# Macaron block on one Trainium2 core: the shared expert moved into the routing stage, routed rows added in a stage of their own, five down passes for the experts

## The reference

```python
x = x + 0.5 * ffn(layernorm(x))
x = x + attention(layernorm(x))
x = x + 0.5 * ffn(layernorm(x))     # the same ffn weights

def ffn(xf):                        # xf: [T, 256]
    scores = sigmoid(xf @ gate_w.T)                 # 8 experts
    w, idx = top_k(scores, 2); w = 2.5 * w / w.sum(-1)
    shared = silu(xf @ shared_wg.T) * (xf @ shared_wu.T) @ shared_wd.T    # 352 hidden units
    h = silu(xf @ exp_wg[e].T) * (xf @ exp_wu[e].T)                       # 176 hidden units per expert
    routed = sum over the two chosen e of w_e * (h @ exp_wd[e].T)
    return shared + routed
```

## Time and profile before

| | us |
|---|---|
| median of 3 runs (lowest, highest) | 1437.1 (1436.49, 1438.13) |
| the profiled execution's own time | 1431.21 |
| its span, first to last instruction | 1429.5 |

### The profile page before, as it was taken

How to read it: one execution, slowest core, us unless ns; L and a number is a source line. 1 busy time by engine, 2 the same in 40 slices (tenths; PEclk the granted TensorE clock), 3 DMA queues, 4 the chain that set the end, 5 groups by cost and what they waited for, 6 DMA issues and landing times. The chain is left out here.

```text
span 1429.5 us, 42640 instructions
## 1 busy us (share of the span) xinstructions
PE 1219.7 (85%) x14356; PEld 938.2 (66%) x14357; DVE 1019.7 (71%) x2317; ACT 770.1 (54%) x1965; POOL 547.7 (38%) x745
## 2 busy tenths in 40 slices
PE   2817999899969849999998999997865299998998
PEld 1516999899958714555554555553743199998998
DVE  6594555479979688898886888981766845554887
ACT  2524556433336504887775777877544156564333
POOL 1555444245524401332332223222535554442554
PEclk9557999999979958999998999999975599998999
DMA  5602433322254492221221222101244034442333
GB/s 184 189 16 76 125 123 122 94 67 73 74 169 166 177 114 52 67 63 59 60 63 49 59 59 64 45 4 35 95 135 135 1 119 124 123 120 76 108 111 106
DMA packets 94745, 132.12 MB, mean 92 GB/s; under 512 B 15040, under 2 KB 79488, under 8 KB 94592
## 3 DMA queue, kind: packets, MB, share of 16 engines
q1 hardware_dynamic: 73088, 85.97, 21.0%
q0 software_dynamic: 13056, 35.67, 9.0%
q10 hardware_dynamic: 8448, 8.39, 1.7%
HBM read 81.35 MB, written 48.23 MB: 91 GB/s over the span
## 5 line engine op out<-in xcount | busy, mean ns | idle before, releaser
L1467 ACT ACTIVATE s_PR<-s_ps_b 128x512 f32<-128x512 f32 (+3 forms) x768 | 331.2, 496 | 144.8 <-PE s_ps_b L1583 139.9
L1489 DVE TENSOR_REDUCE s_MX<-s_ps_a 128x1 f32<-128x512 f32 (+3 forms) x608 | 358.3, 655 | 54.7 <-PE s_ps_a L1558 51.7
L1583 PE MATMUL s_ps_b<-s_QO,s_KO 99*32 99x512 bf16 (+3 forms) x3072 | 220.0, 329 | 9.2 <-issue 4.4
L1443 POOL TENSOR_SCALAR_AFFINE_SELECT s_PR<-s_PR 128x256 f32<-128x256 f32 x256 | 103.0, 405 | 311.6 <-ACT s_PR L1467 305.6
L1558 PE MATMUL s_ps_a<-s_KO,s_QO 96*32 96x512 bf16 (+3 forms) x3072 | 216.4, 339 | 2.7 <-issue 1.7
L604 POOL DMA_INDIRECT f_XG<-xn_scratch,f_tok_u x144 | 136.4, 947 | 165.5 <-PE f_ps_x L701 155.6
L811 POOL DMA_INDIRECT f_YG<-y_scratch,f_slots_u x128 | 121.0, 945 | 143.5 <-DVE X L886 87.9
L1600 PE MATMUL s_ps_o<-s_PR,s_VG 128*17 128x512 f32 (+3 forms) x1536 | 161.1, 488 | 1.0 <-POOL s_PR L1443 0.6
L1583 PEld LDWEIGHTS s_ps_b<-s_QO,s_KO 99*32 99x32 bf16 x3072 | 82.9, 96 | 91.0 <-ACT s_PR L1467 44.7
L657 DVE TENSOR_TENSOR f_xl<-f_ps_x,f_xh 128x256 fp32r<-128x256 f32 x144 | 61.1, 425 | 97.9 <-ACT f_xh L629 97.9
L1558 PEld LDWEIGHTS s_ps_a<-s_KO,s_QO 96*32 96x32 bf16 x3072 | 84.4, 99 | 69.6 <-DVE s_MX L1489 22.7
(11 more groups left out here) (206 smaller groups left out, 3048.9 us busy)
## 6 DMA issues: line engine op xcount, KB each, us to landing
y_scratch<-f_YS SPq DMA_DIRECT2D x144, 128.0 KB, 1.7
qk_scratch<-p_QK SPq DMA_DIRECT2D x32, 384.0 KB, 2.6
s_QO<-qk_scratch SPq DMA_DIRECT2D x96, 128.0 KB, 2.8
s_KO<-qk_scratch SPq DMA_DIRECT2D x96, 128.0 KB, 2.8
xn_scratch<-f_XN ACTq DMA_DIRECT2D x16, 512.0 KB, 3.3
f_stage<-in_w_up SPq DMA_DIRECT2D x20, 352.0 KB
X<-in_x SPq DMA_DIRECT2D x4, 1024.0 KB, 9.4
x_scratch<-X SPq DMA_DIRECT2D x1, 4096.0 KB, 14.8
```

What stands on the lines that cost most here:

```text
L1443: nc.gpsimd.affine_select(out=tile, in_=tile, compare_op=ALU.is_ge, fill=0.0, base=0, pattern=[[0, 2], [1, P]], channel_multiplier=-1)\
L1467: nc.scalar.activation(PR[:, u // 2 % SLOTS, u % 2, 0:W - lo], ps_b[u % RING][:, lo:W], ACT.Exp, scale=SCALE).then_inc(exp_done, 1)
L1489: nc.vector.tensor_reduce(MX[:, h:h + heads, i, s], ps_a[slot][:, 0:heads * keys].rearrange("p (h n) -> p h n", h=heads), AX.X, ALU.max).t ...
L1583: last = nc.tensor.matmul(ps_b[u % RING][strip, lo:W], KO[k][0:RM, h, i * P + strip.start:i * P + strip.stop], QO[k][0:RM, h, hf * W + lo: ...
```

## The change

- The shared expert is computed in the routing stage (now `front_stage`), in the layout "units on partitions, tokens moving": for each wave of four tiles three pieces of 128, 128 and 96 hidden units, each with six passes for gate and six for up of **512 columns** (L716), into a ring of three PSUM banks (`take`). H needs no transposes; ACT and DVE/POOL split it (L381, L339, L507), and nine passes of 256 columns per tile give the result (L730), which DVE adds to X (`add_shared`).
- The gating is spread over waves -1 to 1 (`GATED`), the choice of experts follows in wave 2, the slots in wave 3, and one-hot rounds two to a wave in waves 4 to 7 (`ROWS_AT`). POOL makes no one-hot part any more; ACT makes both (`token_ids`, one instruction of 576 columns and eight of 72).
- The normalised tokens' high and low parts lie in the room of expert w's weights (`x_part`) until wave w's up passes are done; so the weights of expert w are split one wave later (`expert_up`, `expert_down` on ACT, `expert_low` on POOL), from a single staging buffer RAW that SP loads.
- `combine_stage` takes the place of `shared_stage`: only the 64 gathers (ring of eight tiles), two additions per tile, the statistics, and in f2 the stores.
- `expert_stage`: H is cut into 112 and 64 units. The high and the low part of the 64 units lie one above the other on 128 partitions (DVE writes the low part to partitions 64 to 127), and the high weights of those units are kept twice, so low x high and high x high are one pass: five down passes in place of six. DVE makes the low parts in two instructions of 128 columns in place of one of 256.

The core of the diff:

```diff
-        expert_stage(nc, tag, S, ident, WUh, WUl, WDh, WDl, tok_u, unit_i, xn_dram, y_dram)
-        shared_stage(nc, tag, S, X, ST, MV, RSTD, W12, slots_u, ident, WUh, WUl, WSh, WSl, y_dram, out_dram)
+        front_stage(nc, tag, S, X, ST, MV, ident, w_up, w_down, w_shared, gate, xn_dram,
+                    W, RSTD, W12, slots_u, tok_u, unit_i)
+        expert_stage(nc, tag, S, ident, W, tok_u, unit_i, xn_dram, y_dram)
+        combine_stage(nc, tag, S, X, ST, W12, slots_u, y_dram, out_dram)
...
+    GATED = {-1: (0, 1), 0: (2, 3, 4), 1: (5, 6, 7)}
+    LAST_GATED = max(GATED)
+    COUNT_AT = LAST_GATED + 2
+    ROWS_AT = {4: (0, 1), 5: (2, 3), 6: (4, 5), 7: (6, 7)}
...
+            def load_expert(e):
+
+                if e == 0:
+                    sp.wait_ge(shared_lo, 2 + HC)
+                else:
+                    sp.wait_ge(expert_lo, 3 * e)
...
+            for w in range(NW):
+                for m in range(2):
+                    pool.wait_ge(hh_done, HC * w + m + 1)
+                    nc.gpsimd.tensor_tensor(hs[1][:, m, :], H[:, (HC * w + m) % 2, :],
+                                            hs[0][:, m, :].bitcast(F32), ALU.subtract).then_inc(hl_pool, 1)
+                if w >= 1:
+                    expert_low(w - 1)
+            expert_low(NW - 1)
...
+            pe.wait_ge(shared_lo, 2 + HC)
+            for w in range(NW):
+                gated = GATED.get(w, ())
+                up(w, 0)
+                for v in gated[0:1]:
+                    transpose_x(v, 0)
+                    transpose_x(v, 1)
+                for n in ROWS_AT.get(w - 1, ())[1:2]:
+                    tokens(n)
+                if w == COUNT_AT:
+                    counts()
+                if w >= 1:
+                    for i in range(4):
+                        down(w - 1, i)
+                for v in gated[0:1]:
+                    logits(v)
+                for v in gated[1:2]:
+                    transpose_x(v, 0)
+                    transpose_x(v, 1)
+                up(w, 1)
+                for v in gated[0:1]:
+                    turn_logits(v)
+                for v in gated[1:2]:
+                    logits(v)
+                for v in gated[2:3]:
+                    transpose_x(v, 0)
+                    transpose_x(v, 1)
+                up(w, 2)
+                for v in gated[1:2]:
+                    turn_logits(v)
+                for v in gated[2:3]:
+                    logits(v)
+                    turn_logits(v)
+                for n in ROWS_AT.get(w, ())[0:1]:
+                    tokens(n)
+            for i in range(4):
+                down(NW - 1, i)
+            tokens(7)
...
-                plan = split_passes(2)
-                for i, (c, a, b) in enumerate(plan):
-                    last = nc.tensor.matmul(ps_y[k % 2][:, 0:D], hs[a][:, k % 2, c * P:(c + 1) * P],
-                                            W_down[b][c][:, ds((unit - NS) * D, D)],
+                plan = ((hh[0:FA, b, 0:P], S.AH), (hh[0:FA, b, 0:P], S.AL), (hl[:, b, :], S.AH),
+                        (hh[:, b, P:2 * P], S.BH), (hh[0:FB, b, P:2 * P], S.BL))
...
+                if t >= RING:
+                    pool.wait_ge(x_done, t - RING + 1)
```

More of the change, by code:

```diff
@@ L101, in sb @@
             return ctx.enter_context(nc.sbuf_tensor(f"{tag}_{name}", shape, dt))
[L103 to L108, removed]
+        W = sb("W", [P, E, S.BLOCK], F32R)
         RSTD = sb("RSTD", [P, NT])
@@ L437, in _, with place @@
                                                         ALU.mult, ALU.mult))
+            def place():
                 dve.wait_ge(pre_copied, 2)
@@ L537, in _ @@
                 pe.wait_ge(sel_done, 1)
                 pe.wait_ge(consts, 6)
+                take("count", 0)
                 sel = SEL[:, :, :].rearrange("p e t -> p (e t)")
@@ L541, in _ @@
                 nc.tensor.matmul(ps_count[:, 1, :], ones_b[:, :], sel, start=True, stop=True).then_inc(pre_done, 1)
-                for n in range(8):
-                    pe.wait_ge(rows, n + 1)
-                    pe.wait_ge(par_ids, n + 1)
-                    pe.wait_ge(tile_ids, n + 1)
-                    for g in range(CH):
-                        last = nc.tensor.matmul(ps_tok, RSEL[:, n % 2, g, :],
-                                                TSEL[:, n % 2, g, :, :].rearrange("p a j -> p (a j)"),
-                                                start=n == 0 and g == 0, stop=n == 7 and g == CH - 1)
-                    last.then_inc(tok_done, 1)
@@ L553, in feed_forward, with tokens @@
-        expert_stage(nc, tag, S, ident, WUh, WUl, WDh, WDl, tok_u, unit_i, xn_dram, y_dram)
-        shared_stage(nc, tag, S, X, ST, MV, RSTD, W12, slots_u, ident, WUh, WUl, WSh, WSl, y_dram, out_dram)
+            def tokens(n):
+                pe.wait_ge(rows, n + 1)
+                pe.wait_ge(ids, n + 1)
+                for g in range(CH):
+                    last = nc.tensor.matmul(ps_tok, RSEL[:, n % 2, g, :],
+                                            TSEL[:, n % 2, g, :, :].rearrange("p a j -> p (a j)"),
+                                            start=n == 0 and g == 0, stop=n == 7 and g == CH - 1)
+                last.then_inc(tok_done, 1)
@@ L736, in _ @@
             U = 12
+            pe.wait_ge(cleared, 2)
             transpose_x(0, 0)
@@ L988, in attention @@
+                    nc.vector.bn_stats(ST[:, t, :], X[:, t, :])
+            for t in range(NT + 2):
+                if t < NT:
+                    add(t, 0)
+                if 1 <= t <= NT:
+                    add(t - 1, 1)
+                if t >= 2:
+                    statistics(t - 2)
 def attention(nc, S, X, ST, MV, ident, w_qkv, b_qk, b_v, w_out, b_out):
```

1050 lines of the change are left out of this document (531 added, 519 removed).

## The result

| | before | changed |
|---|---|---|
| median of 4 runs, us (lowest, highest) | 1437.62 (1436.49, 1438.33) | 1566.47 (1564.51, 1570.66) |
| ratio, 95% interval | | 1.0901 (1.0875 to 1.0927) |
| profiled execution, us (span) | 1431.21 (1429.5) | 1567.95 (1567.5) |

Slower, as forecast, but by 129 us where I said 82, and 4.5 us above the top of my range. The changed kernel's windows by stage answer to the earlier trace rows; in order: routing, experts and combine of f1, then of f2. Columns: window, its length, busy time of PE, of its weight loads, DVE, ACT and POOL with their counts, clock, DMA share, GB/s.

A forecast was written before the change was run, and what follows sets the result against it. PE was taken to bound the expert and shared stages, DVE chains the routing stage. 175.5 - 16.8 - 76.9 = +81.8 us gave a span of 1511, execution 1513 and, with 5.9 added, median 1519; range 1468 to 1562.

The forecast's parts named there:

- Step 1: Expert stages: one 256-column down pass less in each of 72 tiles at 0.116 us, 8.4 us less per feed-forward.
- rival C: Expert stages: the fifth pass gives nothing because DVE's low parts come late; 16.8 us lost, 1536; chance 0.05.
- Step 2: Combine stage replacing the shared stage, bound by POOL's gathers: 84.7 us in f1 (-38.9), 86.1 in f2 (-38.0).
- Step 3: Routing stage with the shared expert's work: 186.5 us in sum, +88.2 in f1, +87.3 in f2; bounds 150 and 214.
- Waits: Routing stage: PE waiting on chains of other engines, 32 us in sum.
- counts: Routing stage: PE's wait for the choice of experts ahead of the counts, 6 us.
- wave 3 to 4: Routing stage: PE's wait while DVE work stands behind the 11 us slots chain, 9 us.
- rounds: Routing stage: PE's waits for the ids of one-hot rounds 1, 3 and 5, 3 us each, 9 in all.
- Low clock: Routing stage: PE at reduced clock, 4 us at the start and 2 us after its waits.
- The tail: End of the routing stage: 7 us to load and split expert 7, then 1.9 to the first gather; 9 us.
- rival B: Routing stage: the clock falls in the waits, 14 to 30 us more per feed-forward, 1547 to 1579; chance 0.17.
- rival A: Routing stage: the waits are mostly hidden, 20 us less in each feed-forward, 1478; chance 0.18.

The follow-up runs named there:

- plain: Changed kernel with the combine stage's 64 indirect gathers on POOL replaced by 64 plain loads of the same size on SP's queue: 1478.82 us (one run).
- mend: Changed kernel with last down pass padded, PE's 72 expert tiles written out, PE kept busy in routing waits, second raw-weight buffer: 1506.03 us, ratio 1.0464.
- before5: Kernel before with only the experts' down product in five passes, the last over 64 rows: 1461.23 us, ratio 1.0211.
- pad128: Changed kernel with the last down pass of the experts padded with zeros from 64 to 128 rows: 1539.69 us, ratio 1.0746.
- twice64: Changed kernel with the 64-row down pass issued twice in a row: 1584.58 us (one run).
- before5pad: Kernel before with the experts' down product in five passes, the last padded with zeros to 128 rows: 1435.74 us, ratio 1.0034.
- fill: Changed kernel with PE kept busy in its waits of the later routing stage by unused passes of 512 columns: 1551.58 us, ratio 1.0797.
- raw2: Changed kernel with a second buffer for the experts' raw weights, expert e loaded when e - 2 is split: 1555.77 us, ratio 1.0841.
- ring4: Changed kernel with a ring of 4 instead of 8 gathered tiles in the combine stage: 1566.23 us (one run).

## Why the prediction was off

- **Direction and balance: right.** The shared expert's work did not vanish in the idle PE time of the routing stage; it made that stage 90 us longer, and removed from the old shared stage only the part above the gathers. `plain` and `mend` show it from both sides: with the gathers' pace gone the kernel falls by 89 us (and is still 38 above the kernel before), with everything else mended it is still 4.6% slower.
- **Step 1, "-8.4 each": the step that failed.** It measured +15.4 and +16.4. I priced the removed pass by the pitch of 0.12 in the earlier trace rows, a pitch between passes of 88 rows, and took the last pass, over 64 rows, to cost the same. `before5`, `pad128` and `twice64` show that going to 64 rows and back costs 0.2 and 0.18 us by the starts of the loads, 0.34 by the tile outside the loop (2.34 against 2.00), about three passes; less the saved 0.116 a tile is 0.22 longer, 2.34 in place of 2.12. Behind it lay a second error: even without that, PE's queue in the loop holds a tile at 2.24, which leaves nothing of the 8.4 that I forecast (`before5pad`, expert stages 167.9). My rival C gave the fifth pass nothing, but by DVE's low parts; the traces show no wait for them. Of the unknown price I should have said: no row shows a pass of 64 rows, and bounded it from both sides.
- **Step 2, 84.7 and 86.1:** 91.2 and 89.3 here, 85.8 and 86.0 in `pad128`, whose stage differs in nothing. Pace (1.25 us), POOL as the bound and "the deeper ring changes nothing" held. The 5.4 us in f1 are the slow DVE instructions; the 3.3 in f2 lie behind the last addition, at SP. No row of before showed either.
- **Step 3, 186.5:** 190.5 and 187.0 (187.0 to 191.6 in f1 over five executions of this code), right in sum by two errors of opposite sign, which is luck. Waits 32 forecast; in f1 25 measured (all of PE's waits but the first 24.7): counts 4.7 (6), wave 3 to 4 4.2 (9), rounds 2 each (3). Low clock 6 forecast; 35 us of busy PE at half speed cost 17. The tail of 9 was 9.2. So the clock cost 11 us more than I took, where rival B said 14 to 30, and the waits 7 us less, where rival A said 20: a part of each.
- **Own time and median:** I added 5.9 us from before's profile to its median; in the changed kernel the two differ by 1.5 the other way. That alone hid 7 us of the error.

## What to carry to other kernels

A pass saved is worth its pitch only if the passes that replace it have a shape whose pitch the trace shows. A pass over 64 rows between passes over more is to be padded with zeros, and the zeros have to be written somewhere. Not every partial block needs it: in the changed kernel's routing stage the down passes (L730) go from 128 rows to 96 and back at the usual 0.12:

```profile
165.25 0.28 PE L730 MATMUL f_ps_y<-f_WSh,f_hl 128*128 128x256 f32 x1
165.37 0.28 PE L730 MATMUL f_ps_y<-f_WSh,f_hh 96*128 96x256 f32 x1
...
165.60 0.28 PE L730 MATMUL f_ps_y<-f_WSh,f_hl 96*128 96x256 f32 x1
165.72 0.28 PE L730 MATMUL f_ps_y<-f_WSh,f_hh 128*128 128x256 f32 x1
```

When a tile gets shorter, look at what runs beside it and is not shown as busy: here PE's own queue of loads and addresses in a loop was just covered at 2.12 us and became the bound at 2.00. Filling idle time of an engine does not remove the stage that the work leaves, if that stage also covers transfers.

## What the runs showed of the hardware

- A change from a pass over 128 rows to one over 64 and back costs 0.2 us each way (`before5`, `pad128`); changes among 88, 96, 112 and 128 rows cost nothing, and a second 64-row pass costs 0.12 (`twice64`). The Trainium skill, TensorE: Matmul & The Clock Gate, section The mechanism, says in its list that weight loads overlap running matmuls only when the row group differs, but in its first paragraph also names the background weight buffer as a second way. Here loads for all 128 rows start 0.12 us apart beside matmuls over the same rows, and the gap appears just where the rows differ: the measurement decides, against the list. The Trainium skill, TensorEngine Tiling (Array Packing), section When to Use Tiling, counts a contraction of at most 64 rows as a case for two row tiles; a change of the array's arrangement would fit the gap, but no run shows the arrangement itself.
- In a loop over 12 tiles, with an expert number loaded and addresses computed for each, 15 matmuls took 2.22 to 2.24 us, and PE's weight load started 0.05 us after its queue's last register instruction; written out, with the same loads, 2.00.
- DVE took 4.20 us for each three simple instructions, over some 15 of them, and SP 0.7 us each for instructions of 0.02 at the program's end: in both profiles of the changed kernel, in `fill`, `raw2`, `mend` and `ring4`, but not in `pad128` and `twice64` with the same code there. Open.
- Clock: TensorE was granted 1.2 GHz behind two of three waits of 1.9 to 2.1 us (146.8 and 181.0, not 164.12); with PE kept busy through them it stayed at 2.4 GHz. The stretches are not the same in each execution of the same code: PE was busy at 1.2 GHz for 34.5 us of f1's routing stage in the changed kernel, for 26.4 in `ring4`.
